# Local attention in units of two heads and two query blocks

## The reference, cut to what matters

```python
x = x + 0.5 * ffn_ref(layernorm(x))       # 2 layers (below)
x = x + attn_ref(layernorm(x))            # 16 heads, global
x = x + 0.5 * ffn_ref(layernorm(x))
# a layer: 8 heads of 64, blocks of 128 tokens
q, k, v = split(shift_token(x) @ wqkv, 3)
q, k = l2norm(q), l2norm(k); q, k = rotary_xpos(q, k)
# query block i sees key blocks i-1 and i
sim = einsum('bhwid,bhwjd->bhwij', q * 8.0, look_around(k))
attn = softmax(where(mask, -max, sim))
x = x + einsum('bhwij,bhwjd->bhwid', attn, look_around(v)) @ wo
x = x + (a * gelu(g)) @ w2 + b2           # a, g = layernorm(shift_token(x)) @ w1 + b1
```

## Time and profile before

| | us |
|---|---|
| median of 3 runs | 4727.77 |
| lowest and highest run | 4721.86, 4732.27 |
| span of the profiled execution | 4737.6 |
| PE busy in it | 4458.0 (94%) |
| VectorE busy | 2909.6 (61%) |
| ScalarE busy | 2266.2 (48%) |
| GpSimd busy | 2122.0 (45%) |

### The profile page before, as it was taken

How to read it: one execution, slowest core, us unless ns; L and a number is a source line. 1 busy time by engine, 2 the same in 40 slices (tenths; PEclk the granted TensorE clock), 3 DMA queues, 4 the chain that set the end, 5 groups by cost and what they waited for, 6 DMA issues and landing times.

```text
span 4737.6 us, 76538 instructions
## 1 busy us (share of the span) xinstructions
PE 4458.0 (94%) x24256; PEld 3590.7 (76%) x24256; DVE 2909.6 (61%) x7658; ACT 2266.2 (48%) x5384; POOL 2122.0 (45%) x2177
## 2 busy tenths in 40 slices
PE   5899999999999799999999999978999999999998
PEld 4688787878887677777777777756887888778887
DVE  6577767766676355554554554445667667667774
ACT  3455555545555344333333433334555555555553
POOL 3354445434454254444444444433454445444452
PEclk8799999989999899999999999976999899899998
DMA  3000001010000100000000000000000010100000
GB/s 115 13 19 12 17 13 41 17 34 21 18 22 17 38 23 19 1 14 15 1 14 15 1 14 15 19 30 13 12 19 13 17 35 19 34 21 22 18 19 23
DMA packets 101366, 99.90 MB, mean 21 GB/s; under 512 B 11708, under 2 KB 98376, under 8 KB 100936
## 3 DMA queue, kind: packets, MB, share of 16 engines
q1 hardware_dynamic: 100936, 94.66, 6.2%
HBM read 56.91 MB, written 29.36 MB: 18 GB/s over the span
## 4 chain that ended last, share of the span: by engine, by line
PE 68%; issue 9%; DVE 9%; POOL 8%; ACT 3%; DMA 2%; POOLq 0%; SPq 0%; DVEq 0%; ACTq 0%
PE psum L1267 17%; PE psum L1268 14%; PE psum L1269 14%; PE psum L1447 9%; PE psum L1429 5%; PE psum L1525 5%; POOL rinv L571 3%; POOL turned_qk L566 2%; ACT probs L786 1%; DMA nrm<-xmid 1%; PE psum L1504 1%; DVE turned_qk L998 1%; POOL probs L603 1%; POOL pT_lo L583 1%; PE psum L1344 1%
## 5 line engine op out<-in xcount | busy, mean ns | idle before, releaser
L626 POOL TENSOR_TENSOR ge_lo<-ge,ge_hi 128x512 fp32r<-128x512 f32 x512 | 671.1, 1311 | 769.1 <-DVE ge_hi L1191 754.6
L603 POOL TENSOR_SCALAR probs<-probs,rz 128x256 f32<-128x256 f32 (+1 forms) x1024 | 443.3, 452 | 821.9 <-DVE rz L1081 821.9
L842 ACT ACTIVATE ge<-psum 128x512 f32<-128x512 f32 x512 | 306.6, 599 | 820.0 <-PE psum L1525 814.3
L1191 DVE CAST ge_hi<-ge 128x512 fp32r<-128x512 f32 x512 | 228.5, 446 | 677.1 <-ACT ge L842 643.3
L786 ACT ACTIVATE probs<-probs,nb,rq 128x256 f32<-128x256 f32 (+1 forms) x1024 | 575.6, 569 | 23.1 <-DVE nb L1113 20.0
L1447 PE MATMUL psum<-kT,qT 64*128 64x256 f32 (+1 forms) x2048 | 562.9, 429 | 4.6 <-DVE mx L1106 3.2
L1088 DVE TENSOR_TENSOR pT_lo<-psum,pT_hi 128x512 fp32r<-128x512 f32 (+1 forms) x512 | 295.9, 620 | 341.4 <-ACT pT_hi L771 340.2
L1447 PEld LDWEIGHTS psum<-kT,qT 64*128 64x128 f32 x2048 | 390.2, 226 | 104.3 <-issue 43.9
L571 POOL TENSOR_TENSOR rinv<-ssq,minus_half 128x16 f32<-128x16 f32 x128 | 373.7, 2920 | 203.7 <-DVE ssq L991 197.5
L771 ACT CAST pT_hi<-psum 128x512 fp32r<-128x512 f32 (+1 forms) x512 | 252.9, 535 | 387.7 <-PE psum L1429 384.8
L1106 DVE CUSTOM_DVE_ANT_0 probs<-psum,mask 128x256 f32<-128x256 f32 (+1 forms) x1024 | 349.8, 387 | 138.6 <-PE psum L1447 133.7
(11 more groups left out here) (167 smaller groups left out, 12261.8 us busy)
## 6 DMA issues: line engine op xcount, KB each, us to landing
xnext<-stream SPq DMA_DIRECT2D x32, 512.0 KB, 3.9
stream<-xmid SPq DMA_DIRECT2D x16, 512.0 KB, 3.0
nrm<-xmid SPq DMA_DIRECT2D x32, 254.0 KB
x_all<-L_attn_x SPq DMA_DIRECT2D x8, 512.0 KB, 7.5
stream<-x_all SPq DMA_DIRECT2D x8, 512.0 KB, 3.9
nrm<-L_attn_x SPq DMA_DIRECT2D x8, 512.0 KB, 3.9
x_mid<-xmid SPq DMA_DIRECT2D x8, 512.0 KB, 2.9
gx<-x_mid SPq DMA_DIRECT2D x8, 512.0 KB, 4.5
```

The source lines that it names most:

```text
L603: last = nc.gpsimd.tensor_scalar(probs[:, h % 3, i, a:], probs[:, h % 3, i, a:], rz[:, h, i:i + 1], 1.0, ALU.mult, ALU.mult)
L626: nc.gpsimd.tensor_tensor(ges[1][:, k % 4, :], ge[:, k % 4, :], f32(ges[0][:, k % 4, :]), ALU.subtract).then_inc(S["g_lo"], 1)
L842: nc.scalar.activation(ge[:, k % 4, :], RB[k % 2], ACT.Exp, scale=GSCALE, accum_out=gz[:, h, t:t + 1]).then_inc(S["g_exp"], 1)
```

## The change

`unit(u)` turns the eight steps of the slots from heads into units: unit u is both heads of pair u // 2 and the query blocks 0 and 1 (u even) or 2 and 3 (u odd). `RB[side]` and `TB[side]` now belong to one head of the pair and not to one half of the blocks. The orders within a slot become: PE S, T, V, W; ACT E, C, cast of W; DVE `rz`, R, C, subtraction of W. The scores of a unit wait until VectorE has read both sides of the unit before. V is issued for both heads of a pair at once, in the slots 4, 6, 8 and 10, and `pT` holds four heads where it held two. Each unit has four score matmuls and four exponentials, as a head had; a head had 7 transposes, a unit has 6 or 8. The build call also sets `dynamic_dma_scratch_size=1024`.

```diff
+UNITS = HEADS
+def unit(u):
+    pair, half = u // 2, u % 2
+    return (2 * pair, 2 * pair + 1), (2 * half, 2 * half + 1)
+def key_blocks(i):
+    return [j for j in (i - 1, i) if j >= 0]
...
-    pT = [sb(f"pT_{s}", [P, 2, 7 * P], F32R, ffn_mem) for s in ("hi", "lo")]
+    pT = [sb(f"pT_{s}", [P, 4, 7 * P], F32R, ffn_mem) for s in ("hi", "lo")]
...
             for s in range(-1, SLOTS):
+                if s + 1 < UNITS:
+                    u = s + 1
+                    heads, blocks = unit(u)
...
+                        pe.wait_ge(S["dve_s"], 2 * (UNITS * n + u))
+                    for b, i in enumerate(blocks):
+                        a = P if i == 0 else 0
+                        for side in range(2):
+                            rows = slice(side * DH, (side + 1) * DH)
+                            last = mm(RB[side][:, b * 2 * P + a:(b + 1) * 2 * P],
+                                      qT[rows, u // 2, i * P:(i + 1) * P], kT[rows, u // 2, (i - 1) * P + a:(i + 1) * P],
+                                      start=True, stop=True)
+                            if b == 1:
+                                last.then_inc(S["pe_s"], 1)
+                if 0 <= s - 2 < UNITS:
+                    u = s - 2
+                    heads, blocks = unit(u)
+                    pe.wait_ge(S["pool_n"], UNITS * n + u + 1)
...
+                            pe.wait_ge(S["dve_p"], 2 * (UNITS * n + u - 1) + side + 1)
                         col = 0
+                        for b, i in enumerate(blocks):
+                            for j in key_blocks(i):
                                 a = P if i == j else 0
+                                last = turn(TB[side][:, col:col + P], probs[:, u % 3, 2 * side + b, a:a + P], ident[:])
                                 col += P
                         last.then_inc(S["pe_p"], 1)
...
+                if 0 <= s - 4 < UNITS and s % 2 == 0:
+                    p = (s - 4) // 2
...
+                    pe.wait_ge(S["dve_p"], 2 * (UNITS * n + 2 * p + 1) + 2)
+                    for h in (2 * p, 2 * p + 1):
+                        c = (h % 2) * DH
+                        for j in range(NT):
...
+                        last.then_inc(S["pe_av"], 1)
```

On DVE the new R waits for the transposes of three units earlier, as before by `pe_p`; these now stand behind S in PE's list:

```diff
+                        waits = [(S["pe_s"], 2 * (UNITS * n + u) + side + 1)]
+                        if side == 0 and u >= 3:
+                            waits.append((S["pe_p"], 2 * (UNITS * n + u - 2)))
```

More of the change, by code:

```diff
@@ L595, in a_round @@
                     early(n + 1, EARLY[s])
-                h = s - 1
-                if not 0 <= h < HEADS:
+                u = s - 1
+                if not 0 <= u < UNITS:
                     continue
[L600 to L604, removed]
+                need_apart(pool, (S["dve_rz"], UNITS * n + u + 1))
+                heads, blocks = unit(u)
+                for side, h in enumerate(heads):
+                    for b, i in enumerate(blocks):
+                        a = P if i == 0 else 0
+                        pu = probs[:, u % 3, 2 * side + b, a:]
+                        last = nc.gpsimd.tensor_scalar(pu, pu, rz[:, h, i:i + 1], 1.0, ALU.mult, ALU.mult)
                 last.then_inc(S["pool_n"], 1)
@@ L759, in a_round @@
             for s in range(-1, SLOTS):
[L760 to L768, removed]
+                if 0 <= s < UNITS:
+                    act.wait_ge(S["dve_nb"], UNITS * n + s + 1)
+                    if s == 0:
+                        act.wait_ge(S["dve_rq"], n + 1)
+                    heads, blocks = unit(s)
+                    for side, h in enumerate(heads):
+                        for b, i in enumerate(blocks):
+                            a = P if i == 0 else 0
+                            pu = probs[:, s % 3, 2 * side + b, a:]
+                            last = nc.scalar.activation(pu, pu, ACT.Exp, bias=nb[:, h, i:i + 1], scale=rq[:, 0, i, h:h + 1],
+                                                        accum_out=zs[:, h, i:i + 1])
+                    last.then_inc(S["act_exp"], 1)
+                if 0 <= s - 2 < UNITS:
+                    u = s - 2
+                    heads, (i, _) = unit(u)
+                    c, w = (0, 3 * P) if i == 0 else (3 * P, 4 * P)
+                    for side, h in enumerate(heads):
+                        act.wait_ge(S["pe_p"], 2 * (UNITS * n + u) + side + 1)
+                        if u == 0 and side == 0 and f is not None:
                             act.wait_ge(S["pe_w2"], (FJ + 1) * (f + 1))
-                        w = 4 * P if half == 0 else 3 * P
-                        copy(pT[0][:, h % 2, half * 4 * P:half * 4 * P + w], TB[half][:, 0:w]).then_inc(S["act_p"], 1)
+                        if h >= 4:
+                            act.wait_ge(S["pe_av"], HEADS * n + h - 3)
+                        copy(pT[0][:, h % 4, c:c + w], TB[side][:, 0:w]).then_inc(S["act_p"], 1)
                 if s in AV_OUT:
@@ L778, in a_round @@
                     copy(oT[0][:, p % 2, :], PAIR[p % 2]).then_inc(S["act_av"], 1)
[L779 to L789, removed]
                 if s in LATE:
@@ L1077, in a_round @@
             for s in range(-1, SLOTS):
[L1078 to L1088, removed]
+                if 0 <= s - 1 < UNITS:
+                    u = s - 1
+                    hs, ts = slice(u // 2 * 2, u // 2 * 2 + 2), slice(u % 2 * 2, u % 2 * 2 + 2)
+                    dve.wait_ge(S["act_exp"], UNITS * n + u + 1)
+                    V.reciprocal(rz[:, hs, ts], zs[:, hs, ts]).then_inc(S["dve_rz"], 1)
@@ L1089, in a_round @@
+                if 0 <= s - 2 < UNITS:
+                    u = s - 2
+                    heads, (i, _) = unit(u)
+                    c, w = (0, 3 * P) if i == 0 else (3 * P, 4 * P)
+                    for side, h in enumerate(heads):
+                        dve.wait_ge(S["act_p"], 2 * (UNITS * n + u) + side + 1)
+                        V.tensor_tensor(pT[1][:, h % 4, c:c + w], TB[side][:, 0:w], f32(pT[0][:, h % 4, c:c + w]),
                                         ALU.subtract).then_inc(S["dve_p"], 1)
@@ L1094, in a_round @@
                                     ).then_inc(S["dve_av"], 1)
[L1095 to L1113, removed]
                 if s in LATE:
@@ L1411, in a_round @@
             for s in range(-1, SLOTS):
[L1412 to L1417, removed]
+                if s + 1 < UNITS:
+                    u = s + 1
+                    heads, blocks = unit(u)
+                    if u == 0:
+                        pe.wait_ge(S["act_qk"], 2 * NT * (n + 1))
+                        pe.wait_ge(S["act_sq"], 2 * NT * (n + 1))
+                        pe.wait_ge(S["dve_v"], NT * (n + 1))
+                    else:
+                        pe.wait_ge(S["dve_s"], 2 * (UNITS * n + u))
+                    for b, i in enumerate(blocks):
+                        a = P if i == 0 else 0
+                        for side in range(2):
[5 more added lines that the diff above has]
+                                last.then_inc(S["pe_s"], 1)
+                if 0 <= s - 2 < UNITS:
+                    u = s - 2
+                    heads, blocks = unit(u)
+                    pe.wait_ge(S["pool_n"], UNITS * n + u + 1)
+                    for side in range(2):
+                        if u == 0:
                             pe.wait_ge(S["act_qk"], 2 * NT * (n + 1))
@@ L1421, in a_round @@
                         else:
-                            pe.wait_ge(S["dve_p"], 2 * (HEADS * n + h - 1) + half + 1)
+                            pe.wait_ge(S["dve_p"], 2 * (UNITS * n + u - 1) + side + 1)
                         col = 0
[L1424 to L1427, removed]
+                        for b, i in enumerate(blocks):
+                            for j in key_blocks(i):
@@ L1566 @@
     from concourse.bass_utils import run_bass_kernel_spmd
[L1568 removed]
+    nc = bacc.Bacc("TRN2", target_bir_lowering=False, num_devices=1, dynamic_dma_scratch_size=1024)
     arrays, args = {}, []
```

53 lines of the change are left out of this document (20 added, 33 removed).

## The result

| | before | changed |
|---|---|---|
| median, us (4 runs each) | 4730.02 | 4976.51 |
| lowest and highest | 4721.86, 4737.25 | 4974.01, 4979.46 |
| ratio, 95% interval | | 1.0518 [1.0503, 1.0533] |
| span of the profiled execution, us | 4737.6 | 4977.6 |
| mean granted clock of TensorE | 0.935 | 0.926 |

The account below looks back on a forecast made before the run. PE, busy 4458.0 of 4737.6 us, and its two clocks set the end. Per round, 6.0 us saved in S against 11.9 of new waits: +5.9, 189 in 32 rounds, on 4727.8: 4917, rounded to 4915; range 4735 to 5045.

Parts of the forecast that it names:

- The main step: W in slots 5 and 7 loses its cover: PE idle 2 to 3.5 us before it, some 250 us in that group.
- S: the overlap: Scores of both array halves overlap fully: S averages 0.95 us, saving 0.75 a unit, at most 192 us in all.
- starts in issue order: The second side's scores start behind the first's second MATMUL: some 50 us more, about 4965; chance 0.08 shared with no overlap.
- the case of no overlap: S keeps 1.71 us, 6 us a round on top: 5105; chance 0.08 for no overlap or half of it.
- The chain of a round: Attention's steps chained at 2.4 GHz: +5.9 us a round, 189 us; attention of 47 to 48 us at full clock.
- The clock: Falls of PE's clock in attention: no difference taken, ends -134 and +154 us.
- S(3): Scores moved into the 1.37 us idle before T(0), which spoke for fewer clock falls at that place.
- the dearer case: Each gap in slots 5 and 7 makes a whole clock fall: 154 us on top of 189, 5070; chance 0.11.
- The faster case: PE's clock stays up in attention, if gaps come out over 1.7 us a round shorter: 4690; chance 0.14.
- The clock falls more: Rival: gaps in slots 5 and 7 each make a whole fall, 189 + 154 = 343: 5070; chance 0.11.

Follow-up runs that it names:

- e1: The changed kernel with W of pairs 0 to 2 and its casts one slot later (slots 6, 8, 10): 4786.02 us.
- e2: The changed kernel with all score matmuls of one side issued before those of the other, not in turn: 4977.54 us.
- e10: The changed kernel with scores side after side and a small 128-row matmul between the sides, up to slot 5, removing their overlap: 5381.23 us.
- e11: The changed kernel with extra matmuls that change nothing: five ahead of S in slots 2 to 4, and 10, 10, 4 ahead of W in slots 5, 7, 9: 4790.64 us.
- e6: The kernel before with only V moved, both heads of a pair in slots 4, 6, 8 and 10: 4976.79 us.
- e3: The changed kernel with 10, 10 and 4 matmuls that add zero ahead of W's wait in slots 5, 7 and 9: 4905.07 us.
- e4: The changed kernel with ACT's old order in a slot, C and the cast of W ahead of E: 4998.74 us.
- e8: The kernel before with six matmuls, result overwritten, in the idle of 1.37 us ahead of T in slot 2: 4560.53 us.

## Why the prediction was right, and which term was too small

**The main step is shown.** "PE idle of 2 to 3.5 us before W in the slots 5 and 7 ... and some 250 us in that group": 3.45 and 3.13 us, and 282.7. The chain had 3.5, 3.1 and 1.6 for the slots 5, 7 and 9; the last is 1.29. (The first count of this idle in the prediction, 2.4 in the slots 5 and 7, was too small; its sum used the chain.) e1 takes this wait away and 190 us with it.

**S: the overlap** was right: starts 7 ns apart, 0.86 and 1.07 us to T, forecast 0.95 on average. e2 rules out the price for starts in issue order, and e10 the case of no overlap, which costs more than the 5105 that this rival had. But what S saves is more than lost again: at full clock the units, their overlap and the new orders, put on top of V in pairs, cost another 48.8 - 45.8 = 3.0 us a round. S now waits for R of the unit before (204.7 us in all, 3.2 before); how much of that comes from S ahead of T on PE and how much from R ahead of C on DVE was not tried apart.

**The chain of a round is the term that was too small.** The sum gave +5.9 us a round at full clock; e11 shows 48.8 - 41.6 = +7.2, over the 47 to 48 us for attention that were to show the chain right. That is 230 us in 32 rounds, in place of 189; between the kernels it is 218 by the table and 230 as measured, either with the 13 us of e11's five falls in it. Set against the chain, S(4) is 0.2 late (12.7 for 12.5) and S(5) and S(6) 0.6 (16.1 for 15.5, 20.7 for 20.1), since R(4) starts 1.28 us behind the start of T(1), with eight transposes, where 1.0 was chained; in slot 5 T has eight transposes, so that R starts 1.29 us behind T's start where 1.05 was chained, and DVE's C with two halves of 512 takes 1.2 up to the subtraction where 1.05 was chained: W 26.1 for 25.1. Slots 5 to 7 add 0.35 of the same kind, and from there on it is exact (8.2 and 4.2 us for 8.25 and 4.2). The durations of T and C were taken from heads with 7 transposes; those of the odd units, with 8, lie on the path in the slots 3, 5 and 7. With the 0.2 of S(4), which stands ahead of them, this is 1.3 us a round, 41 in all.

**The clock** was forecast as no difference. By the table it is one of 207 - 180 = 27 us, give or take 22; as measured it is 7 to 16, and some 13 more in either case if e11's five falls are counted as clock. So it is small, and not told from none for certain. The reasoning behind it holds only in part. Two shorter falls did take the place of one in eleven rounds. But both costs are larger than the 134 read as 28 falls at 4.8 us: rounds of before with a fall of 10.2 us cost that, others fall for 13.7 us and take 48 in place of 41.6, and the first rounds and those behind the global attention have longer ones still. And S(3), which was to fill the idle of 1.37, leaves other idles of 1.44 and 1.71 ahead of S in the slots 2 to 4, after which 13 rounds still have an early fall. The near parity came out; it isn't shown that it had to, and that this term was so close is in part luck. e6 shows how near the dearer case was: V in pairs without the rest costs 301 - 180 = 121 us more by the clock, as much as by its waits (113).

**The rivals.** The faster case needed gaps over 1.7 us a round shorter than chained; all waits together are 1.3 longer. "The clock falls more" gave 5070 by 154 us more of low clock; there are 27 or fewer by the two ways of reckoning, 40 at most with e11's falls. So of the 246 us over 200 are waits.

**Wrong in expectation:** e3 missed its ranges, e4 and e10 went another way or further than the theory that their range belongs to, each by the clock, which took more than the edit was made to change; e6 and e11 came out 7 and 11 us over, and e8 25 under. The chain by hand told waits to 1.3 us a round; it did not tell where the clock would fall once the spacing changed.

## What to carry to other kernels

Ahead of a matmul whose operand goes through a cast and a subtraction on two other engines, count what the moved work used to cover: here V, and S ahead of it in slot 5, stood in the 3.1 us from T to W, and moving V away cost 113 us of waits alone, and as much again by the clock. Take durations for such a chain from tiles of the size that will stand on the path. And where TensorE's granted clock falls again and again behind one short idle, try full-size matmuls in it before anything else: six of them gave 3.8% here, more than any reordering.

## What the runs showed that was not expected

- Six matmuls of 128x512 in an idle of 1.37 us (1.67 us long, so longer than it) save 179 us (4739.3 to 4560.5). That the idle was what preceded the falls was read in the trace; that filling it would remove nearly all of them was not foreseen to this extent. The runs do not part the idle from the kind of work around it, since the filling changes both.
- Busy is not enough: in e6 the clock stays at 1.2 GHz for 20.5 us in which PE has no pause, with 64-row scores and transposes in turn for the first 15 of them, and comes back at the end of the V behind them.
- Two float32 streams on the two halves of the rows each run at the pace of a single one, 0.21 us from start to start, in either order of issue.
- Serial scores, with the small matmul between them, cost 12.6 us a round, 5 more than the 7.5 by which they are longer at full clock: a longer S also brings more of the low clock.
